# A row maximum moved ahead of an eigenvalue's coefficients, and attention masks added as bf16 products, in a fused four-mixer kernel

## What is computed

```python
# 1: two graph convolutions and, for p = 1..4, an LSTM over windows of p tokens
h = relu(adj @ (h @ Wg0 + bg0)); h = relu(adj @ (h @ Wg1 + bg1)); h = lstm_windows(h)
# 2: graph attention
e = leaky_relu(s1[:, :, None] + s2[:, None, :]); e = where(adj == 0, -inf, e)
out = softmax(e) @ (h @ W)
# 3: one-head attention
scores = q @ k.T / sqrt(128) + adj; scores = where(causal, scores, -1e30)
out = softmax(scores) @ v @ Wo
# 4: spectral network; U are the eigenvectors of the normalized Laplacian of adj
out = U @ (relu(U.T @ h @ W1 + b1) @ W2 + b2)
```

## Time and profile before

| | |
|---|---|
| median of 3 runs | 823.72 us (823.28 to 824.75) |
| the profiled execution | 821.02 us |
| its span, first to last instruction | 819.1 us |
| mean granted TensorE clock | 0.98 |
| TensorE busy | 749.5 us, 91% |
| VectorE busy | 680.4 us, 83% |
| ScalarE busy | 491.3 us, 60% |
| GpSimd busy | 163.0 us, 20% |

### The profile page before, as it was taken

The page is one execution under the profiler, slowest core; times in us unless marked ns, Lnnn a source line. Parts: engine busy times, 40 slices in busy tenths (PEclk is TensorE's granted clock), DMA queues, the critical chain, the costliest instruction groups (busy, mean ns, idle before and its releaser), DMA issues.

```text
span 819.1 us, 13707 instructions
## 1 busy us (share of the span) xinstructions
PE 749.5 (91%) x3718; PEld 500.1 (61%) x3726; DVE 680.4 (83%) x3463; ACT 491.3 (60%) x1115; POOL 163.0 (20%) x379
## 2 busy tenths in 40 slices
PE   3689989999999999999999999759998999697998
PEld 2578864445555566666555555637776777476665
DVE  6898779998888888888888888998898998787533
ACT  0379966664454444444534433529988979497774
POOL 3111112322222211212121221522110210430000
PEclk9999999999999999999999999969999999799999
DMA  9200000000000000000000000000000000000122
GB/s 265 82 2 2 1 1 0 2 1 0 1 1 1 2 0 1 1 1 1 2 1 0 1 0 1 2 0 1 2 1 1 2 1 2 0 2 0 52 78 78
DMA packets 13971, 12.16 MB, mean 15 GB/s; under 512 B 1092, under 2 KB 10823, under 8 KB 13895
## 3 DMA queue, kind: packets, MB, share of 16 engines
q1 hardware_dynamic: 10992, 8.47, 3.5%
q10 hardware_dynamic: 2902, 2.82, 1.2%
HBM read 7.10 MB, written 4.19 MB: 14 GB/s over the span
## 4 chain that ended last, share of the span: by engine, by line
issue 44%; PE 27%; DVE 13%; POOL 12%; ACT 4%; POOLq 0%; DVEq 0%
PE bank L742 24%; POOL col_root L465 8%; POOL XI L469 4%; DVE stat L1003 2%; PE bank L752 2%; DVE X L996 1%; ACT T L693 1%; ACT T L575 1%; ACT T L571 1%; DVE wih L995 1%; DVE HT L995 1%; DVE sm L1144 0%; DVE T L995 0%; DVE tt L995 0%; DVE X L995 0%
## 5 line engine op out<-in xcount | busy, mean ns | idle before, releaser
L635 ACT ACTIVATE G<-bank,bias 128x512 f32<-128x512 f32 (+1 forms) x252 | 158.3, 634 | 172.6 <-PE bank L742 152.4
L742 PE MATMUL bank<-HT,wih 128*128 128x512 f32 (+1 forms) x504 | 243.4, 571 | 0.4 <-ACT HT L621 0.4
L465 POOL TENSOR_TENSOR col_root<-sa,neg_half 128x1 f32<-128x1 f32 x126 | 69.2, 549 | 397.5 <-DVE sa L997 397.5
L742 PE MATMUL bank<-H,whh 128*128 128x512 f32 (+1 forms) x288 | 136.8, 557 | 1.1 <-DVE H L995 0.8
L575 ACT COPY T<-bank 128x512 f32<-128x512 f32 x138 | 80.5, 587 | 53.1 <-PE bank L742 36.2
L571 ACT ACTIVATE T<-X,nbias,rstd 128x128 f32<-128x128 f32 x256 | 104.4, 483 | 7.2 <-DVE nbias L996 7.2
L742 PEld LDWEIGHTS bank<-HT,wih 128*128 128x128 f32 x504 | 80.1, 191 | 14.6 <-issue 8.1
L742 PEld LDWEIGHTS bank<-VI 128*128 128x128 f32 x254 | 45.1, 194 | 68.5 <-DVE VI L995 53.0
L742 PEld LDWEIGHTS bank<-XI,A 128*128 128x128 f32 x252 | 44.2, 194 | 57.2 <-DVE A L996 47.8
L628 ACT ACTIVATE T<-C 128x512 f32<-128x512 f32 (+1 forms) x72 | 41.5, 576 | 30.1 <-DVE C L995 29.9
L752 PE MATMUL bank<-ident,T 128*128 128x128 f32 x256 | 38.7, 281 | 22.6 <-ACT T L693 15.4
(11 more groups left out here) (368 smaller groups left out, 1568.2 us busy)
## 6 DMA issues: line engine op xcount, KB each, us to landing
out_x<-T SPq DMA_DIRECT2D x16, 256.0 KB, 2.3
wih<-in_WihT ACTq DMA_DIRECT2D x1, 1024.0 KB, 12.3
whh<-in_WhhT ACTq DMA_DIRECT2D x1, 1024.0 KB, 18.5
qkvT<-in_WqkvT ACTq DMA_DIRECT2D x1, 192.0 KB
wg<-in_Wg ACTq DMA_DIRECT2D x2, 64.0 KB
l3w<-in_L3W ACTq DMA_DIRECT2D x2, 64.0 KB
adjT<-in_adjT ACTq DMA_DIRECT2D x1, 64.0 KB
adj<-in_adj SPq DMA_DIRECT2D x1, 64.0 KB, 2.0
```

What stands on the lines that cost most here:

```text
L465: e.tensor_tensor(out=col["root"][:, :], in0=sa[:, 0:1], in1=neg_half[:, :], op=ALU.pow).then_inc(root_ready, 1)
L635: e.activation(G[x.h][:, gate, 0:n], gate_bank(k)[:, 0:n], ACT.Tanh if gate == 2 else ACT.Sigmoid, bias=bias[:, 4 * (x.p - 1) + gate:4 * ( ...
L742: mm = lambda out, l, r, start=True, stop=True: e.matmul(out, l, r, start=start, stop=stop)
```

## The change

Four edits.

1. `gmask` is written in bf16. `cmask` stays fp32 while it is formed, and parts 6 to 10 of `masks` then split it into three bf16 tiles `cparts`, each the rest that the one before left, so that their sum is the fp32 value. These parts come in tridiagonal steps 14 to 18.
2. The mask product of a slot is one bf16 product for the graph attention and three for the causal one, with a bf16 identity.
3. The interpolation of the eigenvalue makes two rounds instead of three, clamps once at the end instead of in every round, and folds two clamps of the cell number into one; the selected cell is taken one place to the right and 1 is subtracted at the end.
4. Halves 52 and 53 (the maxima of group 23, and the output of group 22) run after the eigenvalue and before the coefficients; the later halves keep their order. The copies into N2P go to the start of pass 1, before its first two halves, and one copy into CB behind these.

```diff
-        gmask, cmask = sb("gmask", [P, P]), sb("cmask", [P, P])
+        gmask, cmask = sb("gmask", [P, P], BF16), sb("cmask", [P, P])
+        cparts = [sb(f"cpart{i}", [P, P], BF16) for i in range(3)]
...
-                    mask = gmask if nx.gat else cmask
-                    mm(half4(bk[2]), ident[:, :], mask[:, :].unsqueeze(1).to_broadcast([P, GB, P]), stop=False)
+                    for mask in [gmask] if nx.gat else cparts:
+                        mm(half4(bk[2]), identb[:, :], mask[:, :].unsqueeze(1).to_broadcast([P, GB, P]), start=mask is gmask or mask is cparts[0], stop=False)
...
+                if part == 6:
+                    net(e.tensor_copy(out=cparts[0][:, :], in_=cmask[:, :]))
+                if part == 7:
+                    net(TT(cmask[:, :], cmask[:, :], cparts[0][:, :], ALU.subtract))
+                if part == 8:
+                    net(e.tensor_copy(out=cparts[1][:, :], in_=cmask[:, :]))
+                if part == 9:
+                    net(TT(cmask[:, :], cmask[:, :], cparts[1][:, :], ALU.subtract))
+                if part == 10:
+                    net(e.tensor_copy(out=cparts[2][:, :], in_=cmask[:, :]))
...
                     statistics(halves)
+                    link.note(e.tensor_copy(out=N2P[:, :, 0], in_=ne2p[:, 0:P]))
+                    link.note(e.tensor_copy(out=N2P[:, :, 1], in_=ne2p[:, 1:P + 1][:, ::-1]))
                     for _i in range(2):
                         attentions(halves)
                         halves += 1
+                    e.wait_ge(ch_e, link.n)
+                    link.note(e.tensor_copy(out=CB[:, :, 0], in_=N0))
...
-            for _i in range(3):
+            for _i in range(2):
                 link(STT(c("turn"), c("frac"), -1.0, c("frac"), ALU.add, ALU.mult))
                 link(STT(c("frac"), c("turn"), c("bend"), c("frac0"), ALU.mult, ALU.add))
-                link(TS(c("frac"), c("frac"), 0.0, 1.0, ALU.max, ALU.min))
-            link(TT(c("frac"), c("frac"), c("cnt1"), ALU.add))
+            link(TS(c("frac"), c("frac"), 0.0, 1.0, ALU.max, ALU.min))
+            link(TS(c("frac"), c("frac"), c("cnt1"), -1.0, ALU.add, ALU.add))
             STT(c("lam"), c("frac"), c("w"), c("lo"), ALU.mult, ALU.add).then_inc(lam_rdy, 1)
             e.wait_ge(lam_rdy, 1)
-            link(TS(DLP[:, :, 0], d, c("lam"), None, ALU.subtract))
+            for _i in range(2):
+                statistics(halves)
+                attentions(halves)
+                halves += 1
+            link.note(TS(DLP[:, :, 0], d, c("lam"), None, ALU.subtract))
             link(TS(DLP[:, :, 1], d[:, ::-1], c("lam"), None, ALU.subtract))
-            link.note(e.tensor_copy(out=N2P[:, :, 0], in_=ne2p[:, 0:P]))
-            link(e.tensor_copy(out=N2P[:, :, 1], in_=ne2p[:, 1:P + 1][:, ::-1]))
...
-            link.note(e.tensor_copy(out=CB[:, :, 0], in_=N0))
```

More of the change, by code:

```diff
@@ L1322, in _ @@
             TT(QT[:, :], ident[:, :], bank[1][:, 0:P], ALU.subtract).then_inc(wy_dv, 1)
+            by_two = lambda t: t[:, :, :].rearrange("p (s k) c -> p s k c", k=2)
+            D0, D1, N0, N1 = by_two(DLP)[:, :, 0], by_two(DLP)[:, :, 1], by_two(N2P)[:, :, 0], by_two(N2P)[:, :, 1]
             rec = Chain(e, ch_r)
@@ L1420, in _ @@
                     link(e.tensor_reduce(out=c("cnt1"), in_=red[:, 0:f], axis=AX.X, op=ALU.add))
-                link(TS(c("cnt1"), c("cnt1"), 1.0, 1.0, ALU.max, ALU.subtract))
+                    link(TS(c("cnt1"), c("cnt1"), 1.0, float(f - 1), ALU.max, ALU.min))
                 halves += 2
                 if ps < len(POINTS) - 1:
+                    link(TS(c("cnt1"), c("cnt1"), 1.0, 1.0, ALU.max, ALU.subtract))
                     link(STT(c("lo"), c("cnt1"), c("w"), c("lo"), ALU.mult, ALU.add))
@@ L1428, in _ @@
             f = POINTS[-1]
-            link(TS(c("cnt1"), c("cnt1"), float(f - 2), None, ALU.min))
             link(TS(red[:, 0:f], iota_f[:, 0:f], c("cnt1"), None, ALU.is_equal))
             dot = lambda o, a, b, total: e.tensor_tensor_reduce(out=o, in0=a, in1=b, scale=1.0, scalar=0.0, op0=ALU.mult, op1=ALU.add, accum_out=total)
-            link.note(dot(tt[:, 0:f], uu[0][:, 0:f], red[:, 0:f], c("d_at")))
-            link.note(dot(tt[:, 2 * f:3 * f - 1], mx[:, f:2 * f - 1], red[:, 0:f - 1], c("bend")))
-            link(dot(tt[:, f:2 * f - 1], uu[0][:, 1:f], red[:, 0:f - 1], c("d_up")))
+            link.note(dot(tt[:, 0:f - 1], uu[0][:, 0:f - 1], red[:, 1:f], c("d_at")))
+            link.note(dot(tt[:, 2 * f:3 * f - 1], mx[:, f:2 * f - 1], red[:, 1:f], c("bend")))
+            link(dot(tt[:, f:2 * f], uu[0][:, 0:f], red[:, 0:f], c("d_up")))
             link(TT(c("d_up"), c("d_at"), c("d_up"), ALU.subtract))
@@ L1441, in _ @@
             link(TS(c("bend"), c("bend"), -0.5, 0.5, ALU.max, ALU.min))
-            for _i in range(3):
+            for _i in range(2):
                 link(STT(c("turn"), c("frac"), -1.0, c("frac"), ALU.add, ALU.mult))
                 link(STT(c("frac"), c("turn"), c("bend"), c("frac0"), ALU.mult, ALU.add))
-                link(TS(c("frac"), c("frac"), 0.0, 1.0, ALU.max, ALU.min))
-            link(TT(c("frac"), c("frac"), c("cnt1"), ALU.add))
+            link(TS(c("frac"), c("frac"), 0.0, 1.0, ALU.max, ALU.min))
+            link(TS(c("frac"), c("frac"), c("cnt1"), -1.0, ALU.add, ALU.add))
             STT(c("lam"), c("frac"), c("w"), c("lo"), ALU.mult, ALU.add).then_inc(lam_rdy, 1)
             e.wait_ge(lam_rdy, 1)
-            link(TS(DLP[:, :, 0], d, c("lam"), None, ALU.subtract))
+            for _i in range(2):
[3 more added lines that the diff above has]
+            link.note(TS(DLP[:, :, 0], d, c("lam"), None, ALU.subtract))
             link(TS(DLP[:, :, 1], d[:, ::-1], c("lam"), None, ALU.subtract))
-            link.note(e.tensor_copy(out=N2P[:, :, 0], in_=ne2p[:, 0:P]))
-            link(e.tensor_copy(out=N2P[:, :, 1], in_=ne2p[:, 1:P + 1][:, ::-1]))
-            by_two = lambda t: t[:, :, :].rearrange("p (s k) c -> p s k c", k=2)
-            D0, D1, N0, N1 = by_two(DLP)[:, :, 0], by_two(DLP)[:, :, 1], by_two(N2P)[:, :, 0], by_two(N2P)[:, :, 1]
             link.note(TT(CA[:, :, 1], D1, D0, ALU.mult))
             link.note(TT(CB[:, :, 1], D1, N0, ALU.mult))
-            link.note(e.tensor_copy(out=CB[:, :, 0], in_=N0))
             link.note(e.tensor_copy(out=CA[:, :, 0], in_=D0))
-            e.wait_ge(ch_e, link.n - 3)
+            e.wait_ge(ch_e, link.n - 2)
             link(TT(CA[:, :, 1], CA[:, :, 1], N1, ALU.add))
```

## The result

The changed kernel takes 818.48 us (median of 10 runs, 815.54 to 821.09) where the kernel before took 823.54 (10 runs, 820.78 to 824.75): a ratio of 0.994, 95% interval 0.9926 to 0.9955. In a later comparison (e8) it took 816.73 us (6 runs, 813.08 to 819.16), ratio 0.9914 [0.9895, 0.9932]. It is faster by 5 to 7 us, inside the range of 812.4 to 819.8 and 0.7 to 2.5 us above the forecast of 816.0. The first median lies just outside the forecast's own 814.5 to 818, the second inside.

A forecast was written before the change was run, and what follows sets the result against it. VectorE and ScalarE mostly bound the slots, VectorE's chain after the eigenvalue. Gains of 3.4 (masks) - 0.15 (CB copy) + 4.4 (pair and eigenvalue) = 7.65 us take 823.7 to 816.0; own range 814.5 to 818, with rivals 812.4 to 819.8.

The forecast's parts named there:

- Part 1, preparation: Tridiagonal steps 14 to 18: five added mask instructions hide in VectorE's wait for TensorE, cost 0; 1.5 us if uncovered.
- Part 2, mask products: Attention slots: cheaper bf16 mask products shorten X-update waits, 2.3 us in the first mixer plus 1.1 later, 3.4 in all.
- upper bound of part 2: Most the mask products could gain if all seven waits but nothing else of ScalarE stood in the way: 5.6 us.
- Part 3, arithmetic: Eigenvalue interpolation on VectorE: five one-column instructions fewer gain 1.0 us, counted inside the second pivot group's 4.4 us.
- Part 4, the pair: Two halves ahead of the coefficients: second pivot group starts 4.4 us earlier, including 1.0 us of eigenvalue arithmetic.
- second idle: TensorE behind the coefficients: a new 3.0 us idle with a lower-clock restart, making that slot some 2 us dearer.
- The chain's 0.2 us for a busier VectorE: GpSimd's product chain beside a busier VectorE: 0.03 us a block, 0.2 us over all, gain 7.45 instead of 7.65 us.
- The last slots move as a whole: After the second pivot group, the final slots keep the gain already made, the slow restart ready before VectorE asks.
- rival 2: The pair gives little: only mask products and 1.0 us of arithmetic remain, 4.25 us gained, 819.5 us. Chance 0.15.
- Rival 1: Waits for TensorE give way wholly as ScalarE adapts: 10.5 us gained, 813.2 us. Chance 0.15.
- 3 (TensorE bounds all): TensorE limits every slot, so all its saved product time counts: 17.7 us gained, 806 us. Chance 0.02.
- Rival 4: Slower: idles beyond 1.60 to 1.92 us restart TensorE at the lower clock; six restarts give 828 us. Chance 0.06.

The follow-up runs named there:

- e8: The changed kernel, unchanged, measured again in a later comparison: 816.73 us, ratio 0.9914 to the kernel before.
- e9: Kernel before with only the bf16 masks and their preparation, plus 7 and 4 unused TensorE products ending slots 30 and 31: 819.61 us, ratio 0.9952.
- e12: Changed kernel with the causal mask as one fp32 product again, without its three parts and their preparation: 818.43 us, ratio 0.9931 to before.
- e6: Changed kernel plus ten unused bf16 products on TensorE ahead of its 2.63 us idle behind the coefficients: 816.35 us, ratio 0.9911 to before.
- e2: Changed kernel with the old fp32 masks, so eigenvalue arithmetic and pair of halves alone: 817.45 us, ratio 0.9941 to before.
- e4: Changed kernel with only group 23's row maxima ahead of the coefficients, group 22's output half behind them: 817.78 us, ratio 0.9924 to before.
- e11: The kernel before, unchanged, measured and traced a second time: 823.51 us, ratio 1.0003.
- e3: Changed kernel plus 7 and 4 unused bf16 products on TensorE at the ends of slots 30 and 31: 816.85 us, ratio 0.9915 to before.
- e5: Changed kernel with only the row maxima ahead of the coefficients, plus 7 and 4 unused products ending slots 30 and 31: 815.08 us, ratio 0.9893.
- e10: Changed kernel with the old fp32 masks, plus 7 and 4 unused TensorE products ending slots 30 and 31: 818.32 us, ratio 0.9940 to before.
- e1: Kernel before with only the bf16 masks and their preparation: 821.52 us, ratio 0.9991 to before.
- e7: Changed kernel with the old fp32 masks and only group 23's row maxima ahead of the coefficients: 817.16 us, ratio 0.9928 to before.

## Why the prediction was right, and where not

**Part 1, preparation: 0.** Right. In the changed kernel's trace the updates of XI in steps 14 to 18 stand 4.53 us apart, as before, and wait 0.46 to 0.58 us for TensorE. e9, which prepares the parts too, starts the statistics at 537.91 against 537.84 before.

**Part 2, mask products: 3.4 us.** Right against the trace it was made from: 3.40 us at the 22nd update. Within it the graph attention's mask measured 3.1 (e12: the 22nd update at 149.12) and the causal mask 0.3. The waits that I expected at 1 to 2 us in sum are 2.8. Where they are left ScalarE is close to gap-free: two of its opening copies start at 577.40 and 582.79 with no wait shown, 5.39 us apart, and it idles 0.29 us for TensorE between them; I had forecast 5.48 us a slot. The upper bound of part 2 adds up to 5.7 us, not 5.6, which changes nothing else. The price of 0.22 us a bf16 product held (e6).

**Part 3, arithmetic: 1.0 us inside the 4.4.** Right: e2, which has it without the masks, reaches the eigenvalue 0.97 us earlier than before (160.38 - 159.41), although the CB copy, counted at 0.15 us, stands in that stretch.

**Part 4, the pair: 4.4 us.** Right: e2 gains 4.44. The steps hold too, apart from the first idle (0.94 instead of 0.4 us). The second idle was 2.63 us (3.0 forecast), and its slow restart is hidden: with the clock at the higher level the pivot group gains 0.20 us (e6) to 0.31 (e8). GpSimd's chain is the limit by 0.69 us (0.6 forecast); taken off with e4, 0.93 us come back.

The chain's 0.2 us for a busier VectorE is not shown, though. It took 20.09 us in one trace of the kernel before and 20.25 in the other (e11), and 20.29 and 20.02 (e8) in the two of the changed kernel, so two executions of one kernel differ by as much. The rows that I read it from don't carry it either: of the seven distances between block starts in the trace of before, only the fourth and fifth are longer (2.82 and 2.80 us against 2.73 to 2.75), and beside the first block, of 2.74 us, VectorE was busy 2.98 of the 3 us from 705 to 708. The Trainium skill (GPSIMD Engine Reference, Key points), which I cited there, says that GpSimd contends with VectorE's instructions of two SBUF inputs. That this costs the chain anything, no run here shows.

**The step that failed:** "The last slots move as a whole." The last row maximum was early by 7.53 us, the end by 4.70. The 2.8 us between were lost at the lower clock, from 745.5 to 755.8 us, behind the idle ahead of slot 31. I had excluded this by the single row of 1.60 us of idle that was not followed by it, and had not asked what the shorter causal slots do to that idle: it grew to 1.88 us. But the length of the idle isn't what decides. This is how the last two slots looked in all traces (lower clock by windows of 0.1 us):

| trace | idle ahead of slot 31's turn | lower clock in us (after that turn) | last maximum to end |
|---|---|---|---|
| before | 1.60 | none | 69.54 |
| e12 | 1.61 | none | 69.53 |
| e6 | 0.51 | none | 69.59 |
| e3, e5, e9, e10, with fillers | 0.36 at most | none | 69.47 to 69.56 |
| e1 | 1.87 | 749.9 to 753.3 (0.9) | 69.48 |
| e2 | 1.62 | 748.8 to 752.2 (0.9) | 69.53 |
| e4 | 1.87 | 745.1 to 748.5 (1.6) | 69.89 |
| e7 | 1.61 | 745.9 to 749.3 (1.7) | 69.95 |
| e8 | 0.49 | 749.0 to 752.4 (5.6) | 71.16 |
| e11 | 1.62 | 757.0 to 760.4 (6.5) | 71.22 |
| after | 1.88 | 745.5 to 755.8 (0.7) | 72.37 |

So a slow stretch of 3.4 us costs nothing early in slot 31, where the X-update that it delays waits less the next time (e1 waits 2.44 and 0.96 us for its last two, before 1.53 and 1.88). It costs 0.4 us a little later and 1.6 to 1.7 us in slot 32 or behind it, and the 10.3 us of the changed kernel's first trace cost 2.8. (A tail without loss takes 69.5 us, and the cost is what a tail takes beyond that.) Seven of the ten traces without fillers in these slots have a slow stretch there and five lose by it. One of the five is the kernel before (e11), so the loss isn't the change's own. It differs from execution to execution, and the first trace of before was one without it. Why the level stayed low for 10.3 us in one trace and 3.4 in the others stays open. The fillers' worth in the time stays open as well: by the ratios they are worth 3.2 us from e1 to e9, 2.6 from e4 to e5, 2.1 or nothing from the changed kernel's two measurements to e3, and nothing from e2 to e10.

The number owes something to luck. The range reached up to 819.8 us for rival 2, a pair that gives little, and that did not happen; the first median is near that end for another reason.

**The masks' gain in the time.** Of 3.4 to 3.7 us in the traces, most comparisons show less: 0.7 us for the masks alone (0.9991; 4.0 us for e9, whose fillers are in it), 0.1 and 2.2 us more for the two measurements of the changed kernel (0.9940, 0.9914) than for e2 (0.9941), 2.1 more for e3 than for e10, 0.3 more for e4 than for e7. Each of these ratios has an interval of 1 to 2 us to either side, so chance is a part of the spread. Part of the answer may be e11: against this second trace of before the changed kernel of e8 is only 1.82 us ahead at the eighth update (63.88 - 62.06), and 5.35 us at the last row maximum (209.23 - 203.88) instead of 7.84. Both of these traces have the short slow start of 10.2 to 10.3 us, and the first traces of before and after the long one of 13.6 and 13.7, so the masks are worth 1.8 us up to there in the one case and 2.4 in the other. And the sum was made against a trace of before in which the restart at 663.76 was slow, and e11's was not.

Another part may be the clock: e1 ran at a mean granted clock of 0.969 to 0.975, the changed kernel at 0.977 to 0.979 in the first measurement and 0.974 to 0.983 in e8, e2 at 0.981 to 0.985. With the shorter products TensorE idles 1.96 us, 72.49 us after the start of the statistics, where it idled 0.82 before, and in e1, e6 and e8 the lower clock followed (612 to 617 us). That is one of the signs of being wrong that I had named, a new slow stretch between 560 and 690 us, and it came in three of the nine traces with the new masks. In e8's trace it cost the next X-update nothing (77.93 us after the start, 77.95 in the trace of after). Where else the time goes was not found; a profile shows one execution, and the times don't say which stretches were slow in the others.

**The rivals.** Rival 1 (waits give way wholly) and 3 (TensorE bounds all) fall with the 2.8 us of waits that are left and the 3.4 us gained. Rival 2 falls by e2. Rival 4 had the right mechanism in the wrong size: one slow stretch that cost the end 2.8 us in the changed kernel's trace, not four or six restarts of 2.0. Its condition, an idle beyond 1.60 to 1.92 us, does not hold: 1.93 us was followed by the higher clock (e11) and 1.61 by the lower (e7). The Trainium skill's section that I named there (TensorE: Matmul & The Clock Gate, HAM oscillation — how this bites in real kernels) describes bursts that each start slow after a wait. These traces agree only in part: some bursts run slow and some don't, after equal waits of 1.92 and 1.93 us.

**A better version.** e5 has the lowest median, 815.08 us; in the same comparison the changed kernel had 816.73. The intervals of their ratios to before, 0.9879 to 0.9907 and 0.9895 to 0.9932, overlap a little. It has the maxima alone ahead of the coefficients, and eleven products of no use in the last slots. That e5 is faster than the changed kernel is likely from its trace (272.80 us against 275.04 and 276.56 from the statistics on) and not shown by the times.

## What to carry to other kernels

A sum over one trace's waits was good to 0.13 us against the trace that it was made for, up to the point at which a slow stretch of TensorE fell on the path. From there such stretches decided 0 to 2.8 us in each execution. What one costs depends on where it falls and how long it lasts: the same 3.4 us cost between nothing and 1.7. So price a slow stretch near the end as a chance, say which slow stretches the trace behind the sum contains, and ask for a second profile of the unchanged kernel before trusting a difference of under 3 us. Where an engine's chain waits for one value, put ahead of the long computation only that part of the other work which the waiting engine needs: here the row maxima, not the output half (0.93 us in e4's trace, not told apart in its times).

## What the runs showed of the hardware

- The length of an idle time did not tell whether TensorE's lower level (1.2 GHz) followed or the higher (2.4 GHz) stayed: 1.92 us low and 1.93 us high in two traces of one kernel, 2.63 low and 2.65 high in two of another, 1.62 low in e2 and high in e11, 1.32 low in e8 and high in e6. In the last slots the level did not fall during the idle but 0.7 to 2.3 us after TensorE had started again.
- The length of a slow stretch differs as well: 3.4 us for most, 10.3 us in slots 31 and 32 of the changed kernel's first trace; behind the eigenvalue 10.3 us in the first trace of before and 6.8 in e11.
- About 3 us of the time are decided in the first 130 us. The statistics started at 537.84, 537.91 and 537.92 us in three of the 14 traces and at 539.76 to 541.45 in the others. The first three are before, e9 (with the mask parts) and e7 (without), so it isn't the mask parts that decide it. A stretch of 3.4 us at the lower clock that begins at 120.5 to 122.1 us is in ten of the other eleven and in none of these three. It isn't the whole of it: by step 8 (54.59 us in the first trace of before) the changed kernel's first trace is 1.4 us late and e5's 2.4, with the granted clock at 1.00 from 34 to 56 us in both.
